# Attention in a decoder layer: shifted scores as 32-row strip products of 256 columns, without zero-spread query tiles

## The reference

```python
Q = layernorm(query @ Wq.T, gamma, beta); K = layernorm(key @ Wk.T, gamma, beta); V = layernorm(value @ Wv.T, gamma, beta)
# split into 16 heads of 16 features
scores = einsum('bhqd,bhkd->bhqk', Q, K) / sqrt(16)
attn = softmax(scores, axis=-1)
context = einsum('bhqk,bhkd->bhqd', attn, V)
return context @ Wo.T
```

## Time and profile before

| | |
|---|---|
| median of three runs | 1621.47 us (1618.56 to 1626.87) |
| profiled execution | 1620.47 us, of which the span of the trace is 1618.5 us |
| mean granted TensorE clock | 0.875 |
| scan stage | up to about 570 us |
| attention stage | about 573 to 1079 us |
| choice, experts, last norm | the rest |

### The profile page before, as it was taken

The page is one execution under the profiler, slowest core; times in us unless marked ns, Lnnn a source line. Parts: engine busy times, 40 slices in busy tenths (PEclk is TensorE's granted clock), DMA queues, the critical chain, the costliest instruction groups (busy, mean ns, idle before and its releaser), DMA issues. The chain is left out here.

```text
span 1618.5 us, 23462 instructions
## 1 busy us (share of the span) xinstructions
PE 1274.5 (79%) x7183; PEld 900.5 (56%) x7183; DVE 1114.2 (69%) x2401; ACT 744.2 (46%) x1585; POOL 695.8 (43%) x533
## 2 busy tenths in 40 slices
PE   5767777677786759999999998951379999999960
PEld 2222222222232237777887787740369899999950
DVE  4898898999989946666566566558735555545523
ACT  4545455454545335455545545520035555555424
POOL 3566474665646643233222223221533445535430
PEclk8889898998989969899789889865579999999985
DMA  3000000000000012222222222120033344433325
GB/s 105 1 14 1 13 4 9 14 0 13 0 1 1 0 28 63 65 65 65 55 62 65 55 62 68 50 85 1 15 126 56 99 103 86 101 98 66 44 26 208
DMA packets 60733, 80.65 MB, mean 50 GB/s; under 512 B 10209, under 2 KB 52897, under 8 KB 57505
## 3 DMA queue, kind: packets, MB, share of 16 engines
q1 hardware_dynamic: 47808, 58.70, 12.6%
q0 software_dynamic: 12288, 17.05, 6.4%
q10 hardware_dynamic: 576, 4.19, 0.6%
HBM read 42.00 MB, written 21.14 MB: 39 GB/s over the span
## 5 line engine op out<-in xcount | busy, mean ns | idle before, releaser
L489 POOL TENSOR_TENSOR scan_hc<-scan_state,scan_c_sb 128x1024 f32<-128x1024 f32 x128 | 309.0, 2416 | 216.9 <-DVE scan_state L423 201.7
L423 DVE TENSOR_TENSOR_SCAN scan_state<-scan_decay,scan_drive_ps 128x512 f32<-128x512 f32 x256 | 297.2, 1201 | 0.2
L217 PE MATMUL scan_y_ps<-scan_hc,all_ident 128*128 128x512 f32 x520 | 279.3, 664 | 3.1 <-POOL scan_hc L489 3.1
L1602 DVE TENSOR_TENSOR expert_hid_lo<-expert_hid,expert_hid_hi 128x512 fp32r<-128x512 f32 x128 | 88.5, 692 | 177.0 <-ACT expert_hid_hi L1586 162.8
L1499 POOL DMA_INDIRECT acc<-expert_rows,expert_lst x64 | 114.1, 1782 | 179.0 <-DVE expert_rows L1628 164.4
L1581 ACT ACTIVATE expert_hid<-expert_h_ps,expert_b 128x512 f32<-128x512 f32 x128 | 88.2, 689 | 199.9 <-PE expert_h_ps L523 173.3
L320 ACT ACTIVATE scan_decay<-scan_delta,scan_a_neg 128x508 f32<-128x508 f32 x256 | 169.2, 715 | 7.2 <-POOL scan_delta L483 7.2
L348 ACT ACTIVATE scan_c_sb<-scan_c_ps 128x512 f32<-128x512 f32 x128 | 76.6, 598 | 204.6 <-PE scan_c_ps L210 204.6
L416 DVE TENSOR_TENSOR scan_drive_ps<-scan_dx,scan_b_ps 128x512 f32<-128x512 f32 x256 | 162.7, 680 | 8.3 <-PE scan_b_ps L205 3.5
L205 PE MATMUL scan_b_ps<-scan_bcs,scan_sel 96*128 96x512 bf16 x128 | 53.2, 416 | 140.6 <-DVE scan_drive_ps L416 140.6
L217 PEld LDWEIGHTS scan_y_ps<-scan_hc,all_ident 128*128 128x128 f32 x520 | 106.8, 209 | 88.6 <-issue 79.7
(11 more groups left out here) (237 smaller groups left out, 2812.8 us busy)
## 6 DMA issues: line engine op xcount, KB each, us to landing
attn_qz<-attn_q_parts SPq DMA_DIRECT2D x128, 128.0 KB, 2.4
weights_w<-w SPq DMA_DIRECT2D x16, 1024.0 KB
table<-all_row SPq DMA_DIRECT2D x32, 132.0 KB, 1.8
scan_xT<-xT SPq DMA_DIRECT2D x8, 512.0 KB, 4.0
attn_ctxT<-ctxT SPq DMA_DIRECT2D x32, 128.0 KB, 2.5
acc<-all_row SPq DMA_DIRECT2D x32, 128.0 KB, 1.7
final_a<-acc SPq DMA_DIRECT2D x4, 1024.0 KB, 7.1
out<-final_o ACTq DMA_DIRECT2D x4, 1024.0 KB, 5.8
```

The costliest lines, as they stand in the source:

```text
L217: last = pe.matmul(y_ps[k][:], ident[0][:], hc[:, n % RING, k, :], start=False, stop=(n == NS - 1))
L423: dve.tensor_tensor_scan(state[:, n % RING, k, :], decay[:, n % RING, k, :, :].rearrange("p b t -> p (b t)"), drive_ps[k][:], 0.0, ALU.mul ...
L489: pool.tensor_tensor(hc[:, n % RING, :, :], state[:, n % RING, :, :], c_sb[:, n % RING, :].unsqueeze(1).broadcast_to([P, KH, GT]), ALU.mul ...
L1602: dve.tensor_tensor(hid_lo[:, f % RING_H, :], hid[:, f % 2, :], hid_hi[:, f % RING_H, :].bitcast(F32), ALU.subtract).then_inc(hid_ready, 1)
```

## The change

`qz`, its clearing by POOL and its DMAs are taken out. The exact products are done in strips: for each half k of the features, each of the three part pairs and each strip j, a product reads only rows 32j to 32j+31 of the keys and of `q_parts`, 256 columns (the strip's even and odd head), and writes columns 256k to 256k+255 of bank j. The order is strip innermost, as in `scores`. All 24 products of a sequence stand together, ahead of the subtraction for bank 0, and no longer wait for `ntT`; the small products with `pick` stand where `shifted_scores(q, j)` stood. A bank now holds heads 2j, 2j+1, 8+2j and 8+2j+1, and `mix_values` follows that order. SP waits for three clearings in place of five before its loop.

```diff
-        BLANKS = 5
+        BLANKS = 3
@@ sync
-                def spread_queries(q):
-                    sp.wait_ge(m["qk_low"], q.b + 1)
-                    for j in range(4):
-                        rows = slice(32 * j, 32 * j + 32)
-                        sp.dma_start(qz[q.parity][rows, :, :, 2 * j:2 * j + 2, :]...,
-                                     q_parts[q.parity][rows]...).then_inc(qz_moved[q.parity], 16)
@@ gpsimd
-                for i in range(2):
-                    pool.memset(qz[i][:].bitcast(F32), 0.0).then_inc(m["blank_ready"], 1)
@@ tensor
-                def shifted_scores(q, i):
-                    k, h = i // 2, i % 2 * 4
-                    if i == 0:
-                        pe.wait_ge(m["nt_ready"], q.b + 1)
-                        pe.wait_ge(qz_moved[q.parity], 64 * (q.half + 1))
-                        pe.wait_ge(m["qk_low"], q.b + 1)
-                    hi, lo = (qz[q.parity][:, part, k, h:h + 4, :].rearrange("p h t -> p (h t)") for part in range(2))
-                    products(pe, s_ps[i][:], [(k_hi[q.parity][:, k, :], k_lo[q.parity][:, k, :], hi, lo)], True, True)
-                    for c in range(4):
-                        last = pe.matmul(s_ps[i][:, c * P:(c + 1) * P], pick[:, 4 * i + c, :], ntT[:], start=False, stop=True,
-                                         skip_group_check=True)
+                def shifted_scores(q):
+                    pe.wait_ge(m["top_done"], 4 * (q.b + 1))
+                    pe.wait_ge(m["qk_low"], q.b + 1)
+                    for k in range(KH):
+                        for n, (kx, part) in enumerate(((k_hi, 0), (k_hi, 1), (k_lo, 0))):
+                            for j in range(4):
+                                rows = slice(32 * j, 32 * j + 32)
+                                pe.matmul(s_ps[j][:, 2 * k * P:2 * (k + 1) * P], kx[q.parity][rows, k, :],
+                                          q_parts[q.parity][rows, part, k, :, :].rearrange("p e t -> p (e t)"),
+                                          start=(k == 0 and n == 0), stop=False, skip_group_check=True)
+
+                def subtract_top(q, j):
+                    pe.wait_ge(m["nt_ready"], q.b + 1)
+                    for k in range(KH):
+                        for e in range(2):
+                            c = (2 * k + e) * P
+                            last = pe.matmul(s_ps[j][:, c:c + P], pick[:, 8 * k + 2 * j + e, :], ntT[:], start=False, stop=True,
+                                             skip_group_check=True)
                     last.then_inc(m["st_ready"], 1)
@@ mix_values
-                    for h in (2 * pair, 2 * pair + 1):
+                    for n in (2 * pair, 2 * pair + 1):
+                        h = n % 4 // 2 * 8 + n // 4 * 2 + n % 2
@@ step of tensor: where shifted_scores(q, 0) to (q, 3) stood
+                        shifted_scores(q)
+                        subtract_top(q, 0)
+                        subtract_top(q, 1)
+                        subtract_top(q, 2)
+                        subtract_top(q, 3)
```

More of the change, by code:

```diff
@@ L579, in attention_phase @@
         k_lo = [s.sb(f"k_lo{i}", [P, KH, P], F32R) for i in range(2)]
-        qz = [s.sb(f"qz{i}", [P, 2, KH, HEADS // KH, P], F32R) for i in range(2)]
         qb = s.sb("qb", [P, KH, 2, P], BF16)
@@ L615, in attention_phase @@
         ctx_loaded = [s.sem(f"ctx_loaded{i}") for i in range(2)]
-        qz_moved = [s.sem(f"qz_moved{i}") for i in range(2)]
         LOOPED = (NT - 4) // 2
-        BLANKS = 5
+        BLANKS = 3
         def passes(eng, step):
@@ L639, in load_ctx @@
                     sp.dma_start(ctxT[q.parity][:], ctxT_dram[:, :, ds(q.b * SEQ, SEQ)]).then_inc(ctx_loaded[q.parity], 16)
-                def spread_queries(q):
-                    sp.wait_ge(m["qk_low"], q.b + 1)
-                    for j in range(4):
-                        rows = slice(32 * j, 32 * j + 32)
-                        sp.dma_start(qz[q.parity][rows, :, :, 2 * j:2 * j + 2, :].rearrange("p a k e t -> p (a k) (e t)").bitcast(F32),
-                                     q_parts[q.parity][rows].rearrange("p a k e t -> p (a k) (e t)").bitcast(F32)).then_inc(qz_moved[q.parity], 16)
                 def store(q):
@@ L658, in step @@
                         store(q.plus(-2))
-                    if "A" in stages:
-                        spread_queries(q.plus(1))
                 load_ctx(Seq(0, 0))
@@ L780, in mix_values @@
                         pe.wait_ge(m["exp_done"], 4 * q.b + pair // 2 + 1)
-                    for h in (2 * pair, 2 * pair + 1):
-                        last = pe.matmul(o_ps[:, h * (DK + 1):(h + 1) * (DK + 1)], prob[q.parity][:, h, :],
+                    for n in (2 * pair, 2 * pair + 1):
+                        h = n % 4 // 2 * 8 + n // 4 * 2 + n % 2
+                        last = pe.matmul(o_ps[:, h * (DK + 1):(h + 1) * (DK + 1)], prob[q.parity][:, n, :],
                                          v1[q.parity][:, h, :], start=True, stop=True)
@@ L843, in step @@
                     if "B" in stages:
-                        shifted_scores(q, 0)
+                        shifted_scores(q)
+                        subtract_top(q, 0)
                     if "A" in stages:
@@ L847, in step @@
                     if "B" in stages:
-                        shifted_scores(q, 1)
+                        subtract_top(q, 1)
                     if "C" in stages:
@@ L851, in step @@
                     if "B" in stages:
-                        shifted_scores(q, 2)
+                        subtract_top(q, 2)
                     if "C" in stages:
@@ L855, in step @@
                     if "B" in stages:
-                        shifted_scores(q, 3)
+                        subtract_top(q, 3)
                 pe.wait_ge(const.ready, const.steps)
```

## The result

The changed kernel takes 1735.84 us (median of four runs, 1726.25 to 1743.64) against 1620.01 us for the kernel before on the same chip: 1.0717 times as long, with a 95% interval of 1.0632 to 1.0802. The forecast was 1747. The profiled execution took 1730.45 us, its span is 1728.3 us.

A forecast was written before the change was run, and what follows sets the result against it. At 2.4 GHz the ACT and DVE chain bounds the attention period up to project_q, PE the rest. Span 1618.5 + 131 (30 periods, 14.84 to 19.2 us) - 4.6 at the start + 2.0 around it gives 1747 us; range 1595 to 1800.

The forecast's parts named there:

- Strips run four at a time: Shifted scores: 24 strip products cost six rounds of 256 columns, 0.77 us at 2.4 GHz or 1.43 at 1.2, plus 0.1.
- Rival (c): Strips' weight loads run one by one, so 24 take 3.2 us or more; 1670 or 1858 us total; chance 0.13.
- PE's work wasn't the bound at 2.4 GHz: Attention period at 2.4 GHz: ACT and DVE chain holds project_q, so 14.06 us becomes only 13.85, not 11.8.
- the 0.2 us that I kept: Gain per 2.4 GHz period: strips start 0.42 us after the transposed maximum, not 0.77, less 0.1 for strips.
- Rival (d): PE's time is the bound, its 2.3 to 4.2 us per period come off in full; about 1530 us; chance 0.03.
- A period at 1.2 GHz: Attention stage, low clock: 6.7 us to the projection, 4.1 to 4.6 to project_q, 9.6 after; sum 20.7 us.
- The clock stays down: Attention stage: three of four periods low, one recovering at 14.5 us; mean 19.2 us, granted clock 0.55 to 0.7.
- one precedent: Stretch 590.11 to 593.52: strip products, project_q and half of project_kv, PE busy 3.04 us, yet 1.2 GHz was granted.
- The start of the stage: Attention stage start: 3.2 us from the clearing gone, 1.4 us from products fitting PE's idle; 4.6 us won, once.
- The idle before the projection: PE waits for the low part of the mixed values: 2 us and more, about 2.5 us in place of 0.98.
- six rounds: The 24 strip products, four at a time, as 1536 columns; by the skill's rule 0.2 to 0.4 us longer.

The follow-up runs named there:

- e1: Changed kernel with 12 extra full-array products of 256 columns ahead of the output projection, results unread; 1668.95 us.
- e8: Changed kernel with POOL's clearing of two unused query tiles and SP's wait for it put back; 1732.61 us.
- e6: Changed kernel with extra long products: 16 before the projection, 3 before the first mix_values, 6 before project_q, one after each of four later mix_values; 1636.60 us.
- e9: Kernel before, reordered: ACT copies mixed values' high part before its scalings, PE turns them before q and k, projects after the second bank; 1639.18 us.
- e2: Changed kernel with 12 extra products of 16 columns ahead of the output projection; 1714.93 us.

## Why the prediction was right, step by step

- **Strips run four at a time.** Right. 24 products took 1.59 us at 1.2 GHz (1.6 predicted) and 0.91 us at 2.4 (0.87). Rival (c) is out.
- **PE's work wasn't the bound at 2.4 GHz.** Right: 14.04 us between two project_q in e1 for 14.06 before, with PE idle for 1.6 us of it. The gain was smaller than the 0.2 us that I kept: the strips begin 0.57 us after the transposed maximum (906.12 less 905.55), not 0.42, since the four records of mix_values(p,7) take 0.51 us and not 0.36. The way to the projection fell from 5.46 to 5.39 us. Two readings were loose. 14.06 us is the low end of what the kernel before does at 2.4 GHz: ten such periods take 14.05 to 14.81, mean 14.25. And PE's saving there is 2.2 us by the prediction's own terms (3.1 less 0.87), not 2.3. Neither enters the forecast time. Rival (d) is out.
- **A period at 1.2 GHz.** 20.7 predicted, 21.09 measured: 7.05 us to the projection (6.7), 4.76 from there to project_q (4.1 to 4.6), 9.28 to the next maximum (9.6).
- **The clock stays down.** Right in size, 0.62 against 0.55 to 0.7. The make-up was wrong. I let three periods of four stay low throughout and one recover to 14.5 us; measured were eight of 30 low throughout and the rest, but for one, at 17.4 to 18.4 us, in which 2.4 GHz comes twice or, in four, once, a stretch late. The step that failed is that "once the clock has gone down in a mix_values run it stays down for several periods": in most periods 2.4 GHz comes back behind project_q and project_kv, which I had denied on one precedent; in eight it doesn't, and why is open. Two errors offset each other by luck, low periods too many and mixed ones too fast; the mean, 19.2 predicted, was 18.63, which is 17 of the forecast's us. Had the two not offset, the same reasoning would have missed by tens of us, so the mean deserves less trust than its hit suggests.
- **The start of the stage.** 4.6 us predicted, 5.7 measured; the 3.2 us of the clearing measured as 3.4 and shown by e8.
- **The end, and the scan.** Not in the sum: the last two sequences at a low clock, 4.8 us of 7.1 behind the last scores; and a scan stage that ended 5.2 us sooner in this execution. These two nearly cancel, again by luck.
- **The idle before the projection.** "2 us and more" was predicted, and about 2.5 at 2.4 GHz; measured 1.75 us where it is at 1.2 GHz and 1.80 to 2.35 where part of the way is at 2.4. In e6, at 2.4, the gap is 2.6 us, its fillers counted as gap.

By the Trainium skill's 3.07 times for four row tiles (TensorE: Matmul & The Clock Gate, "Measured speedup vs the span model") six rounds were to be 0.2 to 0.4 us longer. This trace doesn't show that for 32x256 fp32r products: 0.91 and 1.59 us from the first strip to the first subtraction, leaving the strips included, against 0.77 and 1.43 for the same columns in full products, so 0.14 and 0.16 us. Entering them doesn't show either: mix_values(p,7) takes 0.51 us before the strips in e6 and 0.53 before a full product in e9 (734.23 to 734.76).

What stays open: how the chip weighs a strip, why some periods stay low throughout, and whether a kernel with strips and other real work in the gaps would hold its clock without paying for fillers.

## What to carry to other kernels

Before taking long matmuls away, look at the granted clock stretch by stretch and ask what PE does right before it rises: here the work that was "wasted" on zeros was what paid for 2.4 GHz, and its price per period (2.2 us of PE time at 2.4 GHz that lay beside a chain anyway) was less than what the lost clock cost (3.8 us). Read the bound of a period at each clock level separately, since a change can be worth nothing at one and steer the share of the other. Short products kept PE busy here but not fast (e2: 520 of 539 us, clock 0.66).

## What the runs showed of the hardware that I had not expected

- The clock's high level can arrive out of step: in the stretches shown of the changed kernel it is granted behind the dense ones, two times out of three for a stretch in which PE had only 1.43 and 1.24 us of work out of 3.41.
- A small DVE instruction can stretch to the end of a POOL instruction that it overlaps: 0.15 to 1.25 us beside POOL's fp32 subtraction (e9), 0.17 to 3.10 us beside its clearing (e8). Over e9's periods DVE is busy 321 us, for 284 before. Not every one does. Just ahead of the 3.10 us, beside the same clearing, e8 has

```profile
577.23 0.15 DVE L46 TENSOR_TENSOR attn_qk_part<-attn_qk_stats 128x2 f32<-128x2 f32 x1
```
- The Trainium skill (SBUF — State Buffer, "SBUF: two separate sides") gives DVE and GpSimd a port pair that one of them holds for its whole instruction: a DVE instruction contends for it in a two-port mode, or with two SBUF inputs against a GpSimd one that reads SBUF. The e9 case has two inputs beside a subtraction, and fits. In e8 the clearing reads nothing: the two-input L46 passes it in 0.15 us, which fits too, and the one-input L48 is held, which fits if it ran in a two-port mode; no row shows its mode.
